# Third group of a routed low-rank layer: a base block and the routing placed earlier in every engine's order

## The reference, cut

```python
# stage 1: bidirectional decayed sums over time (r = x, k = v = f), per channel
ek = exp(min(k, 30)); ekv = ek * v
nf, df = forward_scan(ekv), forward_scan(ek)      # a = a * decay + new
nb, db = backward_scan(ekv), backward_scan(ek)
euk = exp(min(u + k, 30))
y = sigmoid(r) * (nf + nb - ekv + euk * v) / max(df + db - ek + euk, 1e-8) * gain
# stage 2: routed low-rank layer on y, 1024 -> 1024
h = silu(y @ rw1.T + rb1)                         # 64 wide
logits = (h @ rw2.T + rb2)[:, :16] + gates
coeff = softmax over the two best experts, 0 elsewhere
xa = y @ A.T                                      # 16 experts x rank 16 = 256
out = x + y @ W.T + bias + (xa * coeff) @ B.T
```

## Time and profile before

| | |
|---|---|
| time, median of 3 runs | 688.63 us (688.4 to 689.16) |
| profiled execution, its own time | 688.6 us |
| span from first to last instruction | 686.6 us |
| PE busy | 598.7 us, 87% of the span, mean granted clock 0.957 |
| DVE busy | 526.6 us, 77% |
| POOL busy | 368.1 us, 54% |
| ACT busy | 357.1 us, 52% |
| PE idle of 0.5 us and more behind 260.55 us | 1.39, 0.60 and 0.83 us |

### The profile page before, as it was taken

One profiled execution on the slowest core, in us unless ns is written; L12 is line 12 of the kernel. 1 busy time (PEld: TensorE's weight loads), 2 busy tenths in 40 slices (PEclk: granted clock), 3 DMA queues, 4 the chain that ended last, 5 costly groups with the idle time before them and its releaser, 6 DMA issues.

```text
span 686.6 us, 7030 instructions
## 1 busy us (share of the span) xinstructions
PE 598.7 (87%) x2626; PEld 490.1 (71%) x2626; DVE 526.6 (77%) x573; ACT 357.1 (52%) x418; POOL 368.1 (54%) x183
## 2 busy tenths in 40 slices
PE   0153588989999937999999999999999999999997
PEld 0132466768878825887888878888888888888886
DVE  7999999999999999998899797979897532021202
ACT  4777789785656666655655554656465420011000
POOL 1789997867868876647544753565465501000100
PEclk9976799989999978999999999999999999999999
DMA  5323476522945831234423360427132402040022
GB/s 190 122 90 121 124 254 205 194 100 71 215 107 121 203 113 64 74 113 160 141 73 113 109 198 32 153 63 242 33 116 84 124 29 66 27 153 1 25 67 76
DMA packets 33169, 78.42 MB, mean 114 GB/s; under 512 B 4720, under 2 KB 4848, under 8 KB 33136
## 3 DMA queue, kind: packets, MB, share of 16 engines
q1 hardware_dynamic: 30832, 73.79, 33.2%
q0 software_dynamic: 2304, 4.20, 3.8%
HBM read 57.00 MB, written 20.97 MB: 114 GB/s over the span
## 4 chain that ended last, share of the span: by engine, by line
PE 49%; DVE 25%; POOL 16%; issue 7%; ACT 1%; DMA 1%; SPq 0%; DVEq 0%; POOLq 0%; ACTq 0%
PE acc L925 15%; PE acc L927 15%; PE acc L926 15%; DVE mix L713 5%; POOL mix L602 4%; POOL kv L580 4%; POOL yr L586 4%; DVE yr L747 3%; DVE mix L708 3%; DVE eu L723 3%; DVE kv L718 2%; DVE xo L754 2%; POOL y_lo L612 2%; DVE mix L734 2%; PE acc L936 1%
## 5 line engine op out<-in xcount | busy, mean ns | idle before, releaser
L925 PE MATMUL acc<-y_hi,wa_hi 128*128 128x512 f32 x640 | 258.5, 404 | 59.7 <-POOL y_lo L612 52.7
L926 PE MATMUL acc<-y_lo,wa_hi 128*128 128x512 f32 x640 | 255.3, 399 | 0.0
L927 PE MATMUL acc<-y_hi,wa_lo 128*128 128x512 f32 x640 | 254.8, 398 | 0.0
L925 PEld LDWEIGHTS acc<-y_hi,wa_hi 128*128 128x128 f32 x640 | 124.1, 194 | 89.3 <-POOL y_lo L612 54.1
L927 PEld LDWEIGHTS acc<-y_hi,wa_lo 128*128 128x128 f32 x640 | 123.8, 194 | 26.7
L926 PEld LDWEIGHTS acc<-y_lo,wa_hi 128*128 128x128 f32 x640 | 124.2, 194 | 25.6
L602 POOL TENSOR_TENSOR mix<-mix,kv 128x1024 f32<-128x1024 f32 x31 | 74.3, 2397 | 75.7 <-DVE mix L692 59.4
L754 DVE SCALAR_TENSOR_TENSOR xo<-acc,bias_sb,xo 128x512 f32<-128x512 f32 x64 | 46.4, 735 | 75.2 <-PE acc L927 75.2
L612 POOL TENSOR_TENSOR y_lo<-yr,y_hi 128x1024 fp32r<-128x1024 f32 x31 | 74.3, 2398 | 50.2 <-ACT y_hi L402 50.2
L625 POOL TENSOR_TENSOR wx_lo<-xa,wx_hi 128x512 fp32r<-128x512 f32 x16 | 20.9, 1329 | 129.3 <-ACT wx_hi L470 129.3
L580 POOL TENSOR_TENSOR kv<-mix,kv 128x1024 f32<-128x1024 f32 (+1 forms) x32 | 75.4, 2356 | 5.3 <-DVE mix L734 5.3
(11 more groups left out here) (98 smaller groups left out, 738.3 us busy)
## 6 DMA issues: line engine op xcount, KB each, us to landing
kv<-f_cm SPq DMA_DIRECT2D x32, 512.0 KB, 3.6
yr<-x_cm SPq DMA_DIRECT2D x32, 512.0 KB, 3.4
out<-xo SPq DMA_DIRECT2D x64, 256.0 KB, 4.2
xo<-x_cm SPq DMA_DIRECT2D x64, 256.0 KB, 3.9
out<-xo POOLq DMA_DIRECT2D x16, 256.0 KB, 6.8
xa<-w_base SPq DMA_DIRECT2D x5, 512.0 KB, 3.5
xo<-w_base SPq DMA_DIRECT2D x3, 512.0 KB, 5.7
xo<-w_router_a SPq DMA_DIRECT2D x2, 480.0 KB, 3.6
```

The costliest lines, as they stand in the source:

```text
L925: nc.tensor.matmul(out_ap, wh, yh, start=start, stop=False)
L926: nc.tensor.matmul(out_ap, wh, yl, start=False, stop=False)
L927: return nc.tensor.matmul(out_ap, wl, yh, start=False, stop=stop)
```

## The change

For group 2 alone:

- TensorE: block 1 is multiplied beside block 0, unit by unit, so that only block 2 stands behind the logits, and that ahead of the spreads.
- ScalarE, in step 16: `low_rows` ahead of `exp_uk`, then `copy_xa`, the small sigmoid ahead of `sigmoid_r`, `exp_k` of the next unit behind both, `exp_gap`; `split_wx` at the end of step 16.
- VectorE: `hidden` behind the backward denominator scan of step 16; `silu` and `routing` behind `sum_den`; `weigh` at a new place behind `scale_e`, ahead of the backward numerator scan; blocks 0, 1 and 2 evacuated in step 17 instead of 18.
- GpSimd: `split_wx` behind `p1` of step 16.
- SyncE's order is unchanged. All instructions are the same, only their order differs.

```diff
-        hidden_at = {(CB, AFTER_BWD_NUM): 0, (CB + 3, AFTER_SUM): 1}
-        silu_at = {(CB + 1, AFTER_FWD): 0, (CB + 3, AFTER_BWD_NUM): 1}
-        routing_at = {(CB + 1, AFTER_BWD_DEN): 0, (CB + 4, AFTER_FWD): 1}
-        weigh_at = {(CB + 1, AFTER_P2): 0, (CB + 4, AFTER_RATIO): 1}
+        hidden_at = {(CB, AFTER_BWD_NUM): 0, (CB + 3, AFTER_SUM): 1, (2 * CB, AFTER_BWD_DEN): 2}
+        silu_at = {(CB + 1, AFTER_FWD): 0, (CB + 3, AFTER_BWD_NUM): 1, (2 * CB, AFTER_SUM): 2}
+        routing_at = {(CB + 1, AFTER_BWD_DEN): 0, (CB + 4, AFTER_FWD): 1, (2 * CB, AFTER_SUM): 2}
+        weigh_at = {(CB + 1, AFTER_P2): 0, (CB + 4, AFTER_RATIO): 1, (2 * CB, AFTER_SCALE): 2}
...
+                    (2 * CB + 1, AFTER_RATIO): (16, 17), (2 * CB + 1, AFTER_BWD_DEN): (17, 18),
+                    (2 * CB + 1, AFTER_P2): (18, 19)}
...
                 if 0 < s <= UNITS and not late_split:
                     split_hi(s - 1)
+                if second:
+                    low_rows(SPLIT)
                 if s < UNITS:
                     exp_uk(s)
+                if second:
+                    copy_xa(SPLIT)
+                    sigmoid_z(SPLIT)
+                    sigmoid_r(s)
+                    exps()
...
                             base(G, 0, kc - LAG)
-                    for kc in range(CB - LAG, CB):
-                        base(G, 0, kc)
+                            if G == SPLIT:
+                                if kc - LAG == k0:
+                                    bank_in(G, 4)
+                                base(G, 1, kc - LAG)
+                    for j in range(2 if G == SPLIT else 1):
+                        for kc in range(CB - LAG, CB):
+                            base(G, j, kc)
...
-                if G == 0:
-                    pe.wait_ge(xa_copied, 1)
+                if G in (0, SPLIT):
+                    pe.wait_ge(xa_copied, 2 * G + 1)
                     for kc in range(k0, CB):
                         base(G, 2, kc)
```

More of the change, by code:

```diff
@@ L161, in base_from @@
             return HALF if G < SPLIT else 0
-        (AFTER_FWD, AFTER_FWD_NUM, AFTER_RATIO, AFTER_BWD_DEN, AFTER_P2, AFTER_SUM, AFTER_BWD_NUM) = range(7)
-        hidden_at = {(CB, AFTER_BWD_NUM): 0, (CB + 3, AFTER_SUM): 1}
-        silu_at = {(CB + 1, AFTER_FWD): 0, (CB + 3, AFTER_BWD_NUM): 1}
-        routing_at = {(CB + 1, AFTER_BWD_DEN): 0, (CB + 4, AFTER_FWD): 1}
-        weigh_at = {(CB + 1, AFTER_P2): 0, (CB + 4, AFTER_RATIO): 1}
+        (AFTER_FWD, AFTER_FWD_NUM, AFTER_RATIO, AFTER_BWD_DEN, AFTER_P2, AFTER_SUM, AFTER_SCALE, AFTER_BWD_NUM) = range(8)
+        hidden_at = {(CB, AFTER_BWD_NUM): 0, (CB + 3, AFTER_SUM): 1, (2 * CB, AFTER_BWD_DEN): 2}
+        silu_at = {(CB + 1, AFTER_FWD): 0, (CB + 3, AFTER_BWD_NUM): 1, (2 * CB, AFTER_SUM): 2}
+        routing_at = {(CB + 1, AFTER_BWD_DEN): 0, (CB + 4, AFTER_FWD): 1, (2 * CB, AFTER_SUM): 2}
+        weigh_at = {(CB + 1, AFTER_P2): 0, (CB + 4, AFTER_RATIO): 1, (2 * CB, AFTER_SCALE): 2}
         evacs_at = {(CB + 2, AFTER_FWD): (0, 1), (CB + 2, AFTER_FWD_NUM): (1, 2), (CB + 2, AFTER_RATIO): (2, 3),
@@ L494, in _ @@
                 G, q = quarter(s)
-                routed = G >= 0
                 late_split = held(s - 1)
                 new = chunks_at(hi_steps, s)
-                z_of = {CB: 0, CB + 3: 1}.get(s, G if q == 0 else -1)
-                if q == 1:
+                second = s == 2 * CB
+                routed = G > SPLIT
+                z_of = {CB: 0, CB + 3: 1}.get(s, G if q == 0 and routed else -1)
+                if q == 1 and routed:
                     copy_xa(G)
@@ L525, in _ @@
                     exp_k(s + 1)
+                if second:
+                    exp_gap(SPLIT)
                 if s == CB + 1:
@@ L534, in _ @@
                     low_rows(z_of)
-                if s < UNITS:
+                if s < UNITS and not second:
                     sigmoid_r(s)
@@ L540, in _ @@
                     sigmoid_z(z_of)
-                if s < UNITS or z_of >= 0:
+                if (s < UNITS and not second) or z_of >= 0:
                     exps()
@@ L548, in _ @@
                     inverse(s)
+                if second:
+                    split_wx(SPLIT)
                 for n in new:
@@ L652, in _ @@
                     weights_lo(n)
-                if q == 1:
+                if q == 1 and G > SPLIT:
                     split_wx(G)
@@ L664, in _ @@
                     p1(s + 1)
+                if s == 2 * CB:
+                    split_wx(SPLIT)
                 if s == CB - 2:
@@ L915, in _ @@
                     scale_e(s + 1)
+                first_groups(s, AFTER_SCALE)
                 if q == 0 and routed:
@@ L1058, in _ @@
                     logits(G)
-                bank_in(G, 4)
-                for kc in range(k0, CB):
-                    base(G, 1, kc)
-                if G == 0:
-                    pe.wait_ge(xa_copied, 1)
+                if G != SPLIT:
+                    bank_in(G, 4)
+                    for kc in range(k0, CB):
+                        base(G, 1, kc)
+                if G in (0, SPLIT):
+                    pe.wait_ge(xa_copied, 2 * G + 1)
                     for kc in range(k0, CB):
@@ L1068, in _ @@
                     spread(G, a)
-                if G:
+                if G not in (0, SPLIT):
                     for kc in range(k0, CB):
```

2 lines of the change are left out of this document (1 added, 1 removed).

## The result

| | before | changed |
|---|---|---|
| time, median | 688.86 us (5 runs, 688.4 to 689.3) | 699.74 us (5 runs, 699.05 to 699.89) |
| ratio | | 1.0155, 95% interval 1.0144 to 1.0167 |
| span of the profiled execution | 686.6 us | 697.7 us |
| PE, DVE, ACT, POOL busy | 598.7, 526.6, 357.1, 368.1 us | 601.0, 526.5, 357.2, 367.7 us |

A forecast was written before the change was run, and what follows sets the result against it. TensorE and the scan pipeline were taken as tied within a microsecond at 321.77 us, the start of group 3. Scan lag 9.2 plus clock loss 2.2 gave 11.4 us on 688.6: 700.0 us, range 695.5 to 703.

The forecast's parts named there:

- the lag of the scans: VectorE's backward scan of unit 17 starts 9.2 us late, behind routing and weighing, and the delay reaches group 3 in full.
- TensorE's part: Group 2: block 1 partly fills idle stretches, logits come 1.2 us later, experts start 3.1 us earlier, at 282.5.
- The single waits: VectorE, units 16 and 17: idle 5.0 us for the logits, 2.0 for the spreads, 0.5 for the gate.
- The scaling: VectorE, unit 17: falls from 1.55 to 0.74 us since GpSimd isn't busy then, a term of -0.8.
- The evacuations: VectorE, step 17: three evacuations moved ahead of the backward scan of unit 17 add 2.0 us.
- The clock: TensorE, start of group 3: half clock after the long idle costs 2.2 us, bounds 1.8 to 3.4.
- Rival 1: TensorE at unit 15: clock stays full, logits at 268.0, scans' lag 6.9 us, 697.7 us in all; chance 0.15.
- Rival 2 and 3: Four-engine round has slack: scans catch up before block 3, 684.9 us, chance 0.09; or lag just absorbed, 688.6, chance 0.05.
- Rival 4: SyncE's moved loads and stores meet block stores, clock low in more places: 3 to 4 us more, 703.5; chance 0.08.

The follow-up runs named there:

- pe_only: Kernel before with only TensorE's order of the changed kernel, every other engine in the old order; 688.92 us against 688.69, ratio 1.0002.
- evacs_back: Changed kernel with the evacuations of blocks 0 to 2 of the third group back in step 18; 695.37 us, ratio 1.0101.
- filled: Changed kernel with 56 extra matmuls in TensorE's 13 us wait ahead of the third group's last expert product; 697.46 us, ratio 1.0128.
- scan_first: Changed kernel with VectorE's backward numerator scan of unit 16 put ahead of silu, routing and weighing; 699.88 us, ratio 1.0157.
- pool_back: Changed kernel with only GpSimd's split of the weighed products back behind the gate of unit 16; 704.13 us, ratio 1.0222.
- all_three: Changed kernel with unit 16's backward scan ahead of silu, GpSimd's split behind the gate, and evacuations of blocks 0 to 2 in step 18; 692.46 us, ratio 1.0051.

## Why the prediction was right, step by step

The forecast of 700.0 us is 0.3 above the median, and the lag of the scans, its deciding term, was found at every landmark:

| landmark | before | forecast | changed |
|---|---|---|---|
| logits of group 2 | 269.12 | 270.3 | 270.89 |
| first expert of group 2 | 285.64 | 282.5 | 282.58 |
| backward numerator scan, unit 17 | 285.96 | 295.1 | 295.81 |
| evacuation of block 3 | 320.99 | 330.2 | 330.74 |
| start of group 3 on TensorE | 321.77 | 330.9 | 331.52 |
| logits of group 3 | 342.01 | 353.4 | 353.28 |

- **TensorE's part** held: block 1 beside block 0 hides in the idle stretches, experts 3.1 us earlier, and `pe_only` shows that nothing of it reaches the end while the scans set the start of group 3.
- **The lag** was 9.2 forecast and 9.75 to 9.85 measured. The logits came 0.6 us later than worked out, since TensorE stayed at half clock longer from unit 15 on: 0.70 over 10.33 us is 3.1 us lost where the working kept the 2.5 of the kernel before. The single waits were 1.58 and 3.91 us ahead of silu and routing (5.0 forecast, 5.5), 1.54 and 0.20 for the spreads (2.0) and 0.72 for the gate (0.5). The scaling fell to 0.74 as expected. The evacuations cost 2.0, which `evacs_back` shows.
- **The clock** was forecast at 2.2 and cost 1.5 to 1.6 in this execution by the windows; in four other kernels with a long wait at this place it cost 1.8 to 2.6. The lag came out 0.6 too small and the clock 0.7 too large. That the two misses cancel is luck, and it is why the total is closer than its terms.
- **Rival 1** (full clock at unit 15) fell: the burst began at half clock. Its premise of 4.1 to 4.7 us of idle time ahead of it did not hold here, where they were 5.68, but it did in `filled` (4.35) and `pe_only` (4.13), whose TensorE has the same order up to there, and the clock up to the logits was 0.73 and 0.71 in these too. **Rival 2 and 3** (the round has slack) fell with the wait of 5.40 us at the ratio of unit 18, longer than before; the round passed the lag on to within 0.1 us from unit 17 (9.85) to block 3 (9.75). **Rival 4** (a second slip) did not show; the wait at unit 23 is unchanged.
- **What the forecast didn't see** is that VectorE's order was not the only holder. It named GpSimd's sum as waiting for the scan; GpSimd's `split_wx` ahead of the sum would have held it to 282.5 anyway, and once both are undone the early evacuation of block 0 holds the next scan. In the changed kernel the first two run out within 0.13 us of each other, and the third had time to spare, so the sum came out right with one of them counted; that too is luck. As an explanation it was incomplete, and as advice (put the scan first) it would have brought nothing.

The contention that the Trainium skill names (GPSIMD Engine Reference, Specifications) bears on this: in the changed kernel the scaling took 0.74 us with GpSimd idle beside it, against 1.55 in the earlier trace rows, where GpSimd's low half ran from 283.09 to 285.50. What an overlap costs differs: in the kernel before, the scaling at 152.81 took 0.74 us, and it was GpSimd's split beside it (151.62 to 154.69) that took long, 3.07 us against 2.54 at 279.98 above.

## What to carry to other kernels

Where two engines reach a meeting point within a microsecond of each other, work out both arrivals before moving anything; in this kernel time gained on one was lost at the meeting point (`pe_only`), and time lost on the other was lost in full. An engine that executes in order should not get a waiting instruction ahead of work that others wait for, and if that was done on several engines at once, look for all the holders: undoing one of three in a row brought nothing in `scan_first` and made it worse in `pool_back`. When a wait is taken out of a round, look next at what is queued behind the transfer that waited for the same event.

## What the runs showed of the hardware

The stretch at half clock after an idle time varies from execution to execution. `evacs_back` has the changed kernel's order on every engine up to 286 us, and still its matmuls from unit 15 to the logits took 9.21 us at a mean clock of 0.79 (260.49 to 269.70), where the changed kernel took 10.33 us at 0.70 and lost 3.1 us; in the kernel before 2.5 us were lost in the same place. `filled`, also of the same order up to there, took 10.04 us at 0.73. `scan_first` and `all_three` reached the weighing about 1.0 us earlier than the changed kernel with TensorE's order unchanged. A difference of 1 us in a landmark behind a cold start is therefore not one of the kernels. The restart at group 3 varies as much, from 1.5 to 2.6 us lost.
